# A drain of GpSimd's own between the issue of its last output store and the waits for the stores

## The reference

```python
x = x + jnp.tanh(g_xattn[0]) * _L0_xattn_ref(_layernorm(x, axis=-1), ctx_1024, ctx_1024, mask, Wq, bq, Wk, bk, Wv, bv, Wo, bo)
x = x + jnp.tanh(g_ffn[0]) * _L0_ffn_ref(_layernorm(x, axis=-1), W1, b1, W2, b2, Wr, br)

# _L0_ffn_ref: idx = argmax(x @ Wr + br), gates = softmax at idx
for ei in range(e):
    h = jax.nn.gelu(xf @ W1[ei] + b1[ei], approximate=False)
    y = h @ W2[ei] + b2[ei]
    mask = (idxf == ei).astype(xf.dtype)
    out = out + y * (gf * mask)[:, None]
```

## Time and profile before

| | us |
|---|---|
| median of 3 runs | 286.26 |
| lowest, highest | 285.63, 289.72 |
| span of the profiled execution (first to last instruction of the program) | 283.3 |
| median less that span | 3.0 |

### The profile page before, as it was taken

How to read it: one execution, slowest core, us unless ns; L and a number is a source line. 1 busy time by engine, 2 the same in 40 slices (tenths; PEclk the granted TensorE clock), 3 DMA queues, 4 the chain that set the end, 5 groups by cost and what they waited for, 6 DMA issues and landing times.

```text
span 283.3 us, 10494 instructions
## 1 busy us (share of the span) xinstructions
PE 230.7 (81%) x3529; PEld 200.9 (71%) x3529; DVE 190.6 (67%) x639; ACT 166.7 (59%) x482; POOL 182.5 (64%) x222
## 2 busy tenths in 40 slices
PE   1356789998899988888888996788789899999950
PEld 1244678786787876666766785677689799999950
DVE  5547777888998789997779868776575444444310
ACT  2136677797777876677877686345464344444410
POOL 7366756567558889468896886705877655445550
PEclk9999999999999999999999999799999999999995
DMA  7801456536372663316152221233143442110100
GB/s 219 246 16 27 105 151 170 142 85 161 98 207 49 191 161 92 81 37 153 37 155 38 42 51 32 70 86 86 54 135 97 130 120 68 51 34 27 35 21 0
DMA packets 58535, 26.63 MB, mean 94 GB/s; under 512 B 38608, under 2 KB 53989, under 8 KB 58484
## 3 DMA queue, kind: packets, MB, share of 16 engines
q1 hardware_dynamic: 55204, 20.15, 29.3%
q0 software_dynamic: 2272, 4.46, 4.7%
q10 hardware_dynamic: 1008, 1.35, 1.7%
HBM read 16.70 MB, written 5.51 MB: 78 GB/s over the span
## 4 chain that ended last, share of the span: by engine, by line
PE 44%; DVE 17%; POOL 12%; issue 10%; ACT 5%; DMA 4%; SPq 4%; POOLq 0%; DVEq 0%
PE ps L747 13%; PE ps L790 5%; SPq L406 3%; DMA kbd<-kT 3%; DVE mx L1229 3%; PE ps L728 3%; PE ps L805 3%; PE ps L730 3%; PE ps L729 3%; POOL rot L539 2%; POOL rot L545 2%; PE ps L780 2%; PE ps L766 2%; POOL rows L512 2%; POOL rot_s L541 2%
## 5 line engine op out<-in xcount | busy, mean ns | idle before, releaser
L560 POOL DMA_INDIRECT out<-fin,got x39 | 37.9, 972 | 28.2 <-DVE fin L1287 23.4
L1229 DVE TENSOR_REDUCE mx<-ps 128x16 f16<-128x1024 f32 x32 | 39.1, 1221 | 14.6 <-PE ps L805 14.3
L512 POOL DMA_INDIRECT rows<-x_all,dest_i x32 | 33.8, 1057 | 17.1 <-DVE x_all L1064 9.6
L747 PE MATMUL ps<-w_f,hT 128*128 x312 | 44.5, 286 | 0.0
L790 PE MATMUL ps<-vx,pr 128*64 128x32 f32 x1024 | 36.2, 224 | 4.4 <-DVE on L1164 2.4
L747 PEld LDWEIGHTS ps<-w_f,hT 128*128 128x128 f32 x312 | 37.8, 191 | 1.0 <-issue 0.3
L790 PEld LDWEIGHTS ps<-vx,pr 128*64 128x64 f32 x1024 | 32.7, 138 | 8.1 <-issue 2.9
L589 ACT ACTIVATE pr<-ps 128x1024 f32<-128x1024 f32 x32 | 32.7, 1022 | 9.1 <-PE ps L832 8.8
L1287 DVE SCALAR_TENSOR_TENSOR fin<-ps,got 128x128 f32<-128x128 f32 x39 | 13.7, 351 | 35.8 <-PE ps L747 35.6
L539 POOL TENSOR_TENSOR rot<-qk,cf 128x256 f32<-128x256 f32 x32 | 23.5, 733 | 21.3 <-ACT qk L611 15.5
L526 POOL TENSOR_TENSOR stk<-rot,stk 128x256 f16<-128x256 f32 x32 | 21.5, 672 | 21.3 <-DVE stk L1241 21.3
(11 more groups left out here) (158 smaller groups left out, 581.4 us busy)
## 6 DMA issues: line engine op xcount, KB each, us to landing
kbd<-kT SPq DMA_DIRECT2D x128, 32.0 KB
got<-rows SPq DMA_DIRECT2D x39, 72.0 KB, 2.1
w_f<-in_W_rows SPq DMA_DIRECT2D x8, 256.0 KB, 2.9
w_r<-in_W_last_row SPq DMA_DIRECT2D x8, 256.0 KB, 3.1
w_f<-in_L_ffn_W SPq DMA_DIRECT2D x8, 256.0 KB, 5.0
x_all<-in_x SPq DMA_DIRECT2D x3, 512.0 KB, 4.6
xt_all<-in_x_t SPq DMA_DIRECT2D x3, 512.0 KB, 4.5
ct_all<-in_ctx SPq DMA_DIRECT2D x3, 512.0 KB, 4.9
```

The source lines that it names most:

```text
L512: pool.indirect_dma_start(out=rows, out_offset=bass.IndirectOffsetOnAxis(ap=dest_i[:, t:t + 1], axis=0), in_=x_all[:, t, :], in_offset=Non ...
L560: pool.indirect_dma_start(out=out_d, out_offset=bass.IndirectOffsetOnAxis(ap=got_i[:, u % GOT, R_ID:R_ID + 1], axis=0), in_=fin[:, u % FRI ...
L747: mm = pe.matmul(o, hT[:, par, c, :], w2_f[:, bass.ds(e, 1), c, :].rearrange("p o n -> p (o n)"), start=False, stop=(c == FC - 1))
L1229: dve.tensor_reduce(mx[:, t % 2, 0:H], ps_s[:, :].rearrange("p (h k) -> p h k", k=S), AX.X, ALU.max).then_inc(mx_done, 1)
```

## The change

One line is added to GpSimd's program. Between the pipeline, whose last instruction is the issue of the last output store, and the ten waits for the stores to land, GpSimd gets a drain. Nothing is removed and nothing else is moved: the drain at the end of the block stays.

```diff
@@ -563,6 +563,7 @@
                         bounds_check=B * S - 1, oob_is_err=False).then_inc(f_st[pair(u) % (FRING // 2)], 16)
 
             pipeline(step)
+            pool.drain()
             for s in range(FRING // 2):
                 pool.wait_ge(f_st[s], 16 * sum(1 for u in range(NS) if pair(u) % (FRING // 2) == s))
```

## The result

| | before | after |
|---|---|---|
| median, us | 287.01 (20 runs) | 285.35 (20 runs) |
| lowest, highest | 284.75, 290.34 | 282.85, 289.81 |
| ratio to before, with its 95% interval | | 0.9934 [0.9912, 0.9955] |
| span of the profiled execution | 283.3 | 283.5 |
| end of the last descriptors to the end of the span | 7.49 | 6.77 |

The account below looks back on a forecast made before the run. PE paces most of the span, but the tail was put down to POOL's 5.87 us end drain. Landing covered 1.15, less exposed waits 0.28 and second drain 0.17, saves 0.70 us: 286.26 to 285.6, range 284.0 to 287.4.

Parts of the forecast that it names:

- Step 1: The added drain ahead of the waits: 5.87 us from the descriptors' end at 275.80 to 281.67, covering the 1.15 us landing.
- Steps 2 and 3: Behind the added drain: waits and way to the block's drain 0.53 us (0.28 newly exposed), then that second drain 0.17 us.
- B: Both drains at the end cost 5.87 us, a fixed price once GpSimd has used DMAs: 291.3 us, chance 0.14.
- N: The price belongs to the block's end; the added drain ends near 275.85 and all else stays: 286.3 us, chance 0.07.
- D: The added drain's 5.87 us runs from the sequencer's arrival at 274.35, beside the last descriptors: 284.1 us, chance 0.05.
- C: The added drain first waits for the last store's landing at 276.95, then takes 5.87 us: 286.7 us, chance 0.12.

## Why the prediction was right

**The reading of the gap.** It said that three quarters of the 7.5 us behind the last descriptors belong to one drain. (The page shows POOL at 0 in the last slice alone, not in the last slice and a half; nothing hangs on it.) The drains spread over the second part bear that out: they take the block's drain from 5.87 to 0.78 us and the tail from 7.49 to 2.41.

**Step 1, the added drain**, at 5.87 us from the end of the descriptors: measured 282.57 - 276.70 = 5.87. It began 1.47 us before that end (forecast 1.45). The landing, 1.1 us, was the cover. The drain put behind the waits covers none of it, and there the tail stays at 7.39 us.

**Steps 2 and 3.** From the added drain's end to the block's drain it took 283.20 - 282.57 = 0.63 us where 0.53 was put in; the way from the drain's end to the first wait, 0.05 us, was left out, and the rest is spread over the records. The second drain was put at 169 ns and took 43; the row it was taken from had memsets to sit out. The two misses, +0.10 and -0.13 us, nearly cancel, which is luck: 5.87 + 0.63 + 0.04 + 0.23 = 6.77 against the forecast's 6.80.

**The rivals.** B (paid twice) falls by 43 ns here and by 34 ns in the kernel with the drain behind the waits. N (it does nothing of the sort) falls by the same rows. D (from the sequencer's arrival) would have ended the drain at 275.23 + 5.87 = 281.10; it ended at 282.57. Its reason, a fetching of code, which would be paid once, falls too: in the spread kernels five drains of one program cost again each time, and with 91 DMAs the drain cost more than with 71. C (only from the landing) would have been 277.85 + 5.87 = 283.7. But C was half right, as the forecast did not see: a drain does hold for the landing, and by the table above about half of its settling comes behind it. With 71 to settle, the landing at 1.1 us lies wholly under the other half; with 6, 9 or 38 it shows.

**The price by number** was a guess in the forecast, 5.87 / 71 = 0.083 us. With 9, 19, 52, 71 and 91 DMAs it is 0.058 + 0.0818 n, where no landing holds the drain. The forecast did not use it: it costed the added drain at the whole 5.87 and did not ask what a drain elsewhere would bring, which is where 5 us of the tail lay.

**What the sum did not hold.** The first measurement's 0.66% is more than the tail's 0.24%. The two later ones gave 0.24% and none. The drain's gain is as forecast in all three traces of the changed kernel (tail 6.77 us), and it is too small for the ratios to show by themselves; the size of the first ratio beyond it stays open.

## What to carry to other kernels

Read what follows the last busy instruction: the busy tables leave out drains, and here one held 5.87 of 283 us. A drain of GpSimd cost here about 0.08 us for every DMA that GpSimd had issued since its last drain. So for a kernel with many of them, try drains in the middle, where GpSimd has slack, and let the last one find few. Place them where no late landing holds them: one with six DMAs held GpSimd for 2.85 us instead of 0.55. A wait for a landing that stands ahead of a drain with many DMAs to settle adds the landing to the drain's time; with the drain first, the landing was covered. With 9 DMAs that order gained nothing (tail 2.45 against 2.41 us), and leaving the waits out did (1.76).

## What the runs showed of the hardware that was not expected

- A GpSimd drain costs 0.058 + 0.0818 us for each of its own DMAs since the last drain, though all had landed (measured with 9, 19, 71 and 91 of them), the same for a plain one of 32 bytes as for an indirect one of 128 rows.
- It also holds for a store in flight. From the landing to the drain's end it took 0.28 us with 6 DMAs, 0.40 with 9 and 1.60 with 38, about half the price by number, whenever the landing came. With 9 the drain ended 1.53 us after the last descriptors, where the number alone would be 0.79 and the landing stood at 1.13.
- With 52 and 71 DMAs and a store in flight the landing cost nothing: 4.32 and 5.87 us after the engine was free, as by number.
- A drain with no DMA since the last one took 34 to 55 ns.
